# Transposes of values and of x1 moved inside the next projection, with a bank of their own for keys and values

## The chip, the core and the metric

The kernel runs on one core of one Trainium2 chip. The metric is the device time of one execution in microseconds. The kernel before took 1794.83 us (median of three runs, 1790.31 to 1797.67). Of the core's engines, TensorE (PE) multiplies and transposes and writes its results to PSUM, eight banks of 512 fp32 columns. VectorE (DVE) and ScalarE (ACT) read and write PSUM and SBUF, GpSimd (POOL) works in SBUF, and SyncE (SP) issues most DMAs. The engines run their own instruction streams and wait for each other by semaphores.

## The reference

Two layers, each added to its input. With x of shape (8, 512, 512), 16 heads of 64 columns, and one shared head of keys and values:

```python
# layer 0: attention with one head of keys and values
xn = layernorm(x, g_in)
q = (xn @ Wq).reshape(b, n, H, DH).transpose(0, 2, 1, 3) * scale     # Wq: 512 x 1024
k, v = split(xn @ Wkv)                                               # Wkv: 512 x 128
sim = mask(einsum('bhid,bjd->bhij', q, k) + bias)                    # null key and value in front
out = einsum('bhij,bjd->bhid', softmax(sim), v) -> (8, 512, 1024)
x1 = x + layernorm(out @ Wo, g_out)                                  # Wo: 1024 x 512
# layer 1: experts
logits = (x1 @ wt.T + cond @ wg.T) / 2                               # 8 experts, top 2
y = sum of the two chosen experts' outputs, weighted, + shared expert's output
result = x1 + y
```

## The kernel before

The program has stages, one behind the other, with a barrier between: project (to 267 us), attend (to 829 us), output (to 1103 us), then routing, experts and the shared expert. The change touches two of them. Products are made with fp32 operands split into a rounded high part and a rest, so each product is three matmuls (high x high, low x high, high x low).

**Project** (`stage_project`) goes over eight batches b. In SBUF, x of a batch is normalised by VectorE, with GpSimd for the reciprocal deviation. TensorE transposes it (`transpose_x`, L492) into two banks, chunks 0 and 1 first, and 2 and 3 once the banks are free again. ScalarE makes the high part of each chunk (L430), VectorE the rest (L341). Then TensorE makes nine output chunks n of 128 rows, twelve matmuls of 512 columns each (L531 to L533): n = 0 to 7 are queries, n = 8 is keys and values. They go round four banks (`proj_bank[n % 4]`), so keys and values share bank 0 with queries 0 and 4. ScalarE copies a query chunk (`q_hi`, L455), VectorE makes the rest (`q_lo`, L349), and SP stores both; there are two buffers for queries, so the copy of chunk n waits until the stores of chunk n - 2 have landed. ScalarE copies keys and values whole (`kv_out`, L461) and the keys' high part (`k_hi`, L464); VectorE makes `k_lo`. The values are needed transposed: `transpose_v` (L500) does it for batch b - 1 ahead of chunk 0 of batch b, right behind the first half of x's transposes for batch b + 1, and waits for both copies (`kv_copied`). VectorE's `copy_v` puts the result into `values`. The second half of x's transposes stands ahead of chunk 1 (`EARLY`). The masks' and biases' loads are issued by ScalarE between query copies.

**Output** (`stage_output`) goes over 32 tiles t of 128 rows. SP loads a tile of the attention's result (`o_in`), ScalarE and VectorE split it (`oT_hi` L1155, `oT_lo` L1106), and TensorE makes 24 matmuls of 512 columns into one of two banks (`project`, L1189 to L1191). VectorE takes the statistics (L1114, L1117), GpSimd the reciprocal deviation (L1088, L1091), VectorE normalises into `x1` (L1124), GpSimd multiplies by the gain and adds x (L1094, L1097), SP stores. For the logits x1 is transposed (`transpose_x1`, L1207), copied by ScalarE (`copy_x1T`, L1160, one buffer) and multiplied by the router's weights (`route`, L1213, 128 x 8 results). Ahead of the first tiles and of tile 30, ScalarE and VectorE also split the shared expert's weights (L1170, L1129).

All orders here are written by hand: what stands in a row in an engine's code is what it does in a row. TensorE's order of a step in the output stage is

```python
route(t - 2)                 # logits of x1 of tile t - 2
project(t, k)                # 24 matmuls
transpose_x1(t - 1, 1 - k)   # then ScalarE copies, and the next step begins with its route
```

Of the kernel before, what the change touches and what calls it, by code (L numbers as in the profile page):

```python
# [31 lines left out]
H, DH = 16, 64  # L32
# [120 lines left out]
def bank(psum, i):  # L153
    return psum[:, i * BANK:(i + 1) * BANK]
# [19 lines left out]
def stage_project(nc, x, fside, cond, mask, g_in, null_bias, Wq, Wkv, dram, psum, resident, wo_x1, ident, pow_half,  # L174
                  eps, spare, values, null_value):

    with ExitStack() as ctx:
# [42 lines left out]
        NP = IC + 1  # L220
        x_bank = [bank(psum, 0), bank(psum, 1)]
        proj_bank = [bank(psum, 2 + k) for k in range(4)]
        v_bank = bank(psum, 6)
        SMALL = 16 * 4


        EARLY, LATE = 1, 4
        AT_FIRST = (3, 5)

        block = ctx.enter_context(nc.Block())  # L230

# [84 lines left out]
        def _(dve):  # L316
# [46 lines left out]
                                  in1=null_value[:].unsqueeze(1).to_broadcast([P, TB, DH]), op=ALU.subtract  # L363
                                  ).then_inc(v_copied, 1)

            def step(b, k, before=True, split=True, norm=True):
                if split:
                    split_low(b + 1, 1 - k, range(0, 2))
                if before:
                    copy_v(b - 1)  # L370
                lower_q(b, range(0, EARLY))
                if split:
                    split_low(b + 1, 1 - k, range(2, DC))
                lower_q(b, range(EARLY, LATE))
                if norm:
                    measure(b + 2)
                lower_q(b, range(LATE, LATE + 1))
                if norm:
                    shift_and_scale(b + 2)
                lower_q(b, range(LATE + 1, IC))  # L380
                lower_k(b)
# [41 lines left out]
        def _(act):  # L423
# [16 lines left out]
            def copy_q(b, k, biases=None):  # L440
                first = isinstance(b, int) and b == 0
                for n in range(IC):
                    if first and n == 3:

                        act.wait_ge(x_loaded, 32)
                        for i in range(TB):
                            load_biases(i, 0)
                    if biases is not None and n % 4 == 3:
                        load_biases(2 * (1 - k) + n // 4, biases)
                    if n in (AT_FIRST if first else (0, EARLY)) and not (isinstance(b, int) and b + 1 >= B):  # L450
                        split_high(b + 1, 1 - k, range(0, 2) if n == (AT_FIRST[0] if first else 0) else range(2, DC))
                    act.wait_ge(proj_full, NP * b + n + 1)

                    act.wait_ge(q_stored[n % 2], 32 * (IC // 2 * b + n // 2))
                    act.activation(q_hi[:, n % 2, :], proj_bank[n % 4], ACT.Copy, scale=-float(DH) ** -0.5  # L455
                                   ).then_inc(q_hi_ready, 1)
                act.wait_ge(proj_full, NP * b + NP)

                act.wait_ge(vT_full, b)
                act.wait_ge(k_lo_ready, b)  # L460
                act.activation(kv_out[:], proj_bank[IC % 4], ACT.Copy).then_inc(kv_copied, 1)  # L461

                act.wait_ge(k_stored, 32 * b)
                act.activation(k_hi[:], proj_bank[IC % 4][0:DH, :], ACT.Copy).then_inc(kv_copied, 1)  # L464

            for j in range(2):
                act.wait_ge(wq_loaded[j], 16)
# [16 lines left out]
        def _(pe):  # L484
# [9 lines left out]

            def transpose_v(b):

                pe.wait_ge(kv_copied, 2 * b + 2)
                pe.wait_ge(v_copied, b)
                for t in range(TB):
                    last = pe.transpose(v_bank[:, t * P:(t + 1) * P], kv_out[:, t * P:(t + 1) * P], ident[:])  # L500
                last.then_inc(vT_full, 1)

            def project(b, k):
                first, has_next = isinstance(b, int) and b == 0, not (isinstance(b, int) and b + 1 >= B)
                if has_next and not first:
                    transpose_x(b + 1, range(0, 2))
                if not (isinstance(b, int) and b == 0):
                    transpose_v(b - 1)
                pe.wait_ge(xT_lo_ready, DC * b + DC)
                for n in range(NP):  # L510
                    if first and n in (0, IC // 2, IC):

                        pe.wait_ge(weights_lo, (0, IC // 2, IC).index(n) + 1)
                    if first and n == AT_FIRST[0]:
                        transpose_x(b + 1, range(0, 2))
                    if n == (AT_FIRST[1] if first else EARLY) and has_next:
                        transpose_x(b + 1, range(2, DC))

                    if n == 0:
                        pe.wait_ge(kv_copied, 2 * b)  # L520
                    elif n < 4:
                        pe.wait_ge(q_lo_ready, IC * b)
                    else:
                        pe.wait_ge(q_lo_ready, IC * b + n - 3)
                    if n < IC:
                        hi, lo = wq_hi[:, :, n * P:(n + 1) * P], wq_lo[:, :, n * P:(n + 1) * P]
                    else:
                        hi, lo = wkv_hi[:], wkv_lo[:]
                    out = proj_bank[n % 4]
                    for c in range(DC):  # L530
                        pe.matmul(out, hi[:, c, :], xT_hi[k][:, c, :], start=(c == 0), stop=False)  # L531
                        pe.matmul(out, hi[:, c, :], xT_lo[k][:, c, :], start=False, stop=False)
                        last = pe.matmul(out, lo[:, c, :], xT_hi[k][:, c, :], start=False, stop=(c == DC - 1))  # L533
                    last.then_inc(proj_full, 1)
# [423 lines left out]
def stage_output(nc, x, cond, wo_stage, wo_loaded, g_out, wt, wg, sw_gate, sw_up, sw_down, shared, dram, psum, ident,  # L958
                 pow_half, eps, spare, logits, x1_in, x1_loaded):

    with ExitStack() as ctx:
# [37 lines left out]
        WO_PARTS = [(0, 4), (4, IC)]  # L999

        WO_STARTS = [lo for lo, hi in WO_PARTS]

        SPLIT_AT = {0: 0, 1: 1, T - 2: 2}

# [144 lines left out]
        def _(act):  # L1149
# [12 lines left out]
            def step(t, k, m):  # L1162
                if not (known(t) and t + 1 >= T):
                    split_high(t + 1, 1 - k, m + k)
                if not (known(t) and t == 0):
                    copy_x1T(t - 1)
                if known(t) and t in SPLIT_AT:
                    n = SPLIT_AT[t]
                    act.wait_ge(shared_loaded[n], 16)
# [4 lines left out]
                act.activation(wo_hi[:, lo:hi, :], wo_part(j), ACT.Copy).then_inc(wo_hi_ready, 1)  # L1174
            split_high(0, 0, 0)
            steps(act, step)
            copy_x1T(T - 1)

        @block.tensor
        def _(pe):  # L1180
            def project(t, k):
                pe.wait_ge(oT_lo_ready, 2 * t + 2)
                if not (known(t) and t < 2):

                    pe.wait_ge(y_ready, t - 1)
                for c in range(IC):
                    if known(t) and t == 0 and c in WO_STARTS:
                        pe.wait_ge(wo_lo_ready, WO_STARTS.index(c) + 1)
                    pe.matmul(out_bank[k], oT_hi[k][:, c, :], wo_hi[:, c, :], start=(c == 0), stop=False)  # L1189
                    pe.matmul(out_bank[k], oT_hi[k][:, c, :], wo_lo[:, c, :], start=False, stop=False)  # L1190
                    last = pe.matmul(out_bank[k], oT_lo[k][:, c, :], wo_hi[:, c, :], start=False, stop=(c == IC - 1))  # L1191
                last.then_inc(out_full, 1)

            def group_logits():

# [19 lines left out]
                last.then_inc(logits_full, 1)  # L1215

            def step(t, k, m):
                if not (known(t) and t < 2):
                    route(t - 2)
                project(t, k)  # L1220
                if not (known(t) and t == 0):
                    transpose_x1(t - 1, 1 - k)
                if known(t) and t == 1:
                    group_logits()

            steps(pe, step)
            route(T - 2)
            transpose_x1(T - 1, 1)
            route(T - 1)
# [874 lines left out]
```

## Time and profile before

| | |
|---|---|
| runs | 1790.31, 1794.83, 1797.67 us |
| profiled execution, its own time | 1795.32 us |
| its span | 1793.6 us, mean clock of TensorE 0.967 |
| PE busy | 1631.7 us (91%), 10364 matmuls |
| DVE, ACT, POOL busy | 974.2, 714.9, 730.2 us |
| project stage, 53 to 267 us | PE busy 196.1 of 214 us |
| output stage, 866 to 1095 us | PE busy 206.06 of 229 us |

Matmuls are pipelined, so their durations overlap: the start of one to the start of the next is what it costs TensorE. The waits tell where it stands still and for whom. The granted clock is 1.00 at 2.4 GHz and 0.5 at 1.2 GHz; a stretch between has both.

### The profile page before, as it was taken

To read this page: it belongs to the slowest core of one execution; us is meant where nothing else is said; L and a number is where in the kernel's file an instruction comes from. 1 tells how busy PE (TensorE), PEld (TensorE's weight loads), DVE (VectorE), ACT (ScalarE), POOL (GpSimd) and SP (SyncE) were. 2 spreads that over 40 slices of the span, in tenths; PEclk is the share of its full clock that TensorE was granted. 3 is DMA by queue.
4 is the path that set the end of the run, shared out by engine and by line. 5 is a ranking of instruction groups with operands and counts; after the bars stand their busy time and mean duration, and the time that the engine had idled before them with its cause. 6 is when DMAs were issued, how large, how long until landed. Compare 5 with 4: busy or idle time off the path is not lost. (4 is left out here: it accounts for less than half of the span.)

```text
span 1793.6 us, 36160 instructions
## 1 busy us (share of the span) xinstructions
PE 1631.7 (91%) x10364; PEld 1362.8 (76%) x10365; DVE 974.2 (54%) x2442; ACT 714.9 (40%) x1823; POOL 730.2 (41%) x1177
## 2 busy tenths in 40 slices
PE   6899996999999999996988987989999999999998
PEld 4677775888888888885777776777777788778886
DVE  5444525776676676775554554653333333356555
ACT  3222324776676676774222121213333343321221
POOL 1000234675576676674554553142222222134222
PEclk9999998999999999998999998989999999989999
DMA  6566657776776766775444344015446633246333
GB/s 214 192 224 203 225 209 211 214 218 181 210 209 183 214 199 181 212 215 148 147 134 136 128 134 153 0 55 203 176 147 268 217 108 108 88 119 216 111 100 112
DMA packets 172361, 301.32 MB, mean 168 GB/s; under 512 B 16658, under 2 KB 64322, under 8 KB 170196
## 3 DMA queue, kind: packets, MB, share of 16 engines
q1 hardware_dynamic: 142324, 235.21, 41.1%
q0 software_dynamic: 11200, 35.73, 6.9%
q10 hardware_dynamic: 18720, 29.12, 4.7%
q8 instruction: 37, 0.61, 0.1%
q14 instruction: 80, 0.66, 0.1%
HBM read 186.99 MB, written 113.00 MB: 167 GB/s over the span
## 5 line engine op out<-in xcount | busy, mean ns | idle before, releaser
L754 POOL TENSOR_SCALAR probs<-probs,rsums 128x512 f32<-128x512 f32 (+3 forms) x512 | 264.0, 532 | 203.8 <-DVE rsums L790 203.4
L782 DVE CUSTOM_DVE_ANT_0 scores<-psum,resident 128x514 f32<-128x514 f32 (+3 forms) x512 | 243.2, 484 | 158.8 <-PE psum L897 136.9
L855 ACT ACTIVATE probs<-scores,lowest 128x514 f32<-128x514 f32 (+3 forms) x512 | 284.2, 557 | 34.1 <-DVE lowest L782 33.1
L909 PE MATMUL psum<-ident,probs 128*128 128x128 f32 x1280 | 235.1, 283 | 21.3 <-DVE probsT L797 14.0
L897 PE MATMUL psum<-keys,queries 128*128 (+4 forms) x640 | 222.6, 356 | 23.8 <-DMA queries_and_ones<-q_hi_d 17.8
L909 PEld LDWEIGHTS psum<-ident,probs 128*128 128x128 f32 x1280 | 152.3, 142 | 54.4 <-issue 39.5
L897 PE MATMUL psum<-keys_lo_and_mask,queries_and_ones 128*128 (+4 forms) x640 | 185.2, 298 | 0.0
L929 PE MATMUL psum<-probsT,v_now 128*64 128x128 f32 x2560 | 168.3, 278 | 0.9 <-DVE probsT L797 0.9
L897 PEld LDWEIGHTS psum<-keys,queries 128*128 128x128 f32 x640 | 127.7, 199 | 35.0 <-issue 21.0
L864 ACT ACTIVATE probsT<-psum 128x512 f32<-128x512 f32 (+2 forms) x192 | 93.6, 487 | 137.7 <-PE psum L909 120.2
L929 PEld LDWEIGHTS psum<-probsT,v_now 128*64 128x64 f32 x2560 | 137.4, 137 | 14.4 <-issue 1.6
L1806 PE MATMUL psum<-expert_weights,xT_hi 128*128 x284 | 122.4, 431 | 4.5 <-SPq L1694 4.0
L897 PEld LDWEIGHTS psum<-keys_lo_and_mask,queries_and_ones 128*128 128x128 f32 x640 | 125.8, 197 | 0.0
L797 DVE COPY probsT<-psum 128x512 f32<-128x512 f32 (+1 forms) x192 | 121.8, 635 | 3.8 <-PE psum L909 3.1
L1189 PE MATMUL psum<-wo_hi,oT_hi 128*128 128x512 f32 x256 | 105.2, 411 | 11.3 <-DVE oT_lo L1106 11.3
L1766 DVE TENSOR_TENSOR hT_lo<-psum,hT_hi 128x256 fp32r<-128x256 f32 x71 | 30.1, 424 | 157.0 <-ACT hT_hi L1723 157.0
L1808 PE MATMUL psum<-expert_weights,xT_lo 128*128 x284 | 112.8, 397 | 0.0
L1807 PE MATMUL psum<-expert_weights,xT_hi 128*128 x284 | 112.5, 396 | 0.0
L349 DVE SCALAR_TENSOR_TENSOR q_lo<-psum,q_hi 128x512 fp32r<-128x512 f32 x64 | 43.9, 687 | 125.2 <-ACT q_hi L455 125.2
L455 ACT ACTIVATE q_hi<-psum 128x512 fp32r<-128x512 f32 x64 | 38.3, 598 | 173.5 <-DMA q_lo_d<-q_lo 104.3
L531 PE MATMUL psum<-xT_hi,wq_hi 128*128 128x512 f32 x256 | 105.1, 411 | 1.6 <-DVE xT_lo L341 1.6
L138 POOL COPY slot_rows<-slot_tokens 128x1 int32 (+1 forms) x71 | 13.0, 183 | 224.0 <-PE psum L1801 221.6
(240 smaller groups left out, 3696.1 us busy)
## 6 DMA issues: line engine op xcount, KB each, us to landing
ys_d<-y_out ACTq DMA_DIRECT2D x71, 256.0 KB, 2.0
q_hi_d<-q_hi SPq DMA_DIRECT2D x64, 256.0 KB, 2.5
q_lo_d<-q_lo SPq DMA_DIRECT2D x64, 256.0 KB, 2.9
queries<-q_hi_d SPq DMA_DIRECT2D x64, 256.0 KB, 3.7
queries<-q_lo_d SPq DMA_DIRECT2D x64, 256.0 KB, 4.2
queries_and_ones<-q_hi_d SPq DMA_DIRECT2D x64, 256.0 KB, 4.5
oT_d<-o_out SPq DMA_DIRECT2D x64, 256.0 KB, 2.2
o_in<-oT_d SPq DMA_DIRECT2D x32, 512.0 KB, 3.9
```

What stands on the lines that cost most here:

```text
L531: pe.matmul(out, hi[:, c, :], xT_hi[k][:, c, :], start=(c == 0), stop=False)
L754: pool.tensor_scalar(out=row, in0=row, scalar1=rsums[:, n % RING:n % RING + 1], scalar2=1.0, op0=ALU.mult, op1=ALU.mult).then_inc(probs_sc ...
L782: dve.tensor_tensor_reduce(out=scores[n % 4][:, 0:CK[i]], in0=score_psum(n), in1=bias_of(resident, i, h), scale=1.0, scalar=3.0e38, op0=AL ...
L797: dve.tensor_copy(dst, src).then_inc(probsT_odd, 1)
L855: act.activation(probs[n % RING][:, 0:CK[i]], scores[n % 4][:, 0:CK[i]], ACT.Exp, bias=lowest[:, n % 4:n % 4 + 1], scale=-1.0, accum_out=s ...
L897: last = pe.matmul(whole[:, lo:hi], qs[hp % 2][:, n % 2, i * P:(i + 1) * P], ks[:, bass.ds((b % 2) * (AHEAD + S) + lo, hi - lo)], start=(p ...
L909: last = pe.transpose(probsT_bank[g % 2][:, at + j * P:at + (j + 1) * P], probs[n % RING][:, AHEAD + j * P:AHEAD + (j + 1) * P], ident[:])
L929: last = pe.matmul(o_bank[hp % 2][head * DH:(head + 1) * DH, cols], v_now[:, j * DH:(j + 1) * DH], probsT[half][:, at:at + P], start=(j == ...
L1189: pe.matmul(out_bank[k], oT_hi[k][:, c, :], wo_hi[:, c, :], start=(c == 0), stop=False)
L1806: pe.matmul(out, hi, experts[:, bass.ds(at, D)], start=start, stop=False)
L1807: pe.matmul(out, hi, experts[:, bass.ds(at + EW, D)], start=False, stop=False)
L1808: return pe.matmul(out, lo, experts[:, bass.ds(at, D)], start=False, stop=stop)
```

## The change

In the projection stage the transposes of batch b - 1's values go from the front of batch b to behind its second chunk (`VALUES_AT = 2`), and they wait for the first of the two key and value copies alone. Keys and values get bank 7. The waits for banks are written anew: a query chunk waits for the chunk that held its bank, across the batch's border too. VectorE's `copy_v` moves from the front of its step to behind the lowering of chunk 1.

In the output stage a tile's 24 matmuls are cut after 6 and after 15. In the first cut stand the transposes of x1 of tile t - 2 (before: of tile t - 1, behind the tile), in the second the logits of tile t - 2. ScalarE's copy follows. Behind the last tile come the transposes and logits of the last two.

```diff
-        v_bank = bank(psum, 6)
+        v_bank, kv_bank = bank(psum, 6), bank(psum, 7)
+        VALUES_AT = 2
 # VectorE, project stage
-                if before:
-                    copy_v(b - 1)
                 lower_q(b, range(0, EARLY))
                 if split:
                     split_low(b + 1, 1 - k, range(2, DC))
-                lower_q(b, range(EARLY, LATE))
+                lower_q(b, range(EARLY, VALUES_AT))
+                copy_v(b - 1)
+                lower_q(b, range(VALUES_AT, LATE))
 # ScalarE, project stage
-                act.activation(kv_out[:], proj_bank[IC % 4], ACT.Copy).then_inc(kv_copied, 1)
+                act.activation(kv_out[:], kv_bank, ACT.Copy).then_inc(kv_copied, 1)
-                act.activation(k_hi[:], proj_bank[IC % 4][0:DH, :], ACT.Copy).then_inc(kv_copied, 1)
+                act.activation(k_hi[:], kv_bank[0:DH, :], ACT.Copy).then_inc(kv_copied, 1)
 # TensorE, project stage
-                pe.wait_ge(kv_copied, 2 * b + 2)
+                pe.wait_ge(kv_copied, 2 * b + 1)
...
-                if not (isinstance(b, int) and b == 0):
-                    transpose_v(b - 1)
...
-
-                    if n == 0:
+                    if n == VALUES_AT and not (isinstance(b, int) and b == 0):
+                        transpose_v(b - 1)
+
+                    if n == IC:
                         pe.wait_ge(kv_copied, 2 * b)
-                    elif n < 4:
-                        pe.wait_ge(q_lo_ready, IC * b)
-                    else:
+                    elif not (isinstance(b, int) and b == 0 and n < 4):
                         pe.wait_ge(q_lo_ready, IC * b + n - 3)
...
-                    out = proj_bank[n % 4]
+                    out = proj_bank[n % 4] if n < IC else kv_bank
 # output stage
+        CUTS = [range(0, 2), range(2, 5), range(5, IC)]
 # ScalarE
-                if not (known(t) and t == 0):
-                    copy_x1T(t - 1)
+                if not (known(t) and t < 2):
+                    copy_x1T(t - 2)
...
             steps(act, step)
+            copy_x1T(T - 2)
             copy_x1T(T - 1)
 # TensorE; project() takes the chunks it makes, waits at the first and signals at the last
-            def project(t, k):
+            def project(t, k, chunks):
...
             def step(t, k, m):
+
+                project(t, k, CUTS[0])
+                if not (known(t) and t < 2):
+                    transpose_x1(t - 2, k)
+                project(t, k, CUTS[1])
                 if not (known(t) and t < 2):
                     route(t - 2)
-                project(t, k)
-                if not (known(t) and t == 0):
-                    transpose_x1(t - 1, 1 - k)
+                project(t, k, CUTS[2])
                 if known(t) and t == 1:
                     group_logits()
 
             steps(pe, step)
+            transpose_x1(T - 2, 0)
             route(T - 2)
             transpose_x1(T - 1, 1)
             route(T - 1)
```

TensorE at the border of two batches before, from the last matmul of keys and values on (line, operation, output and inputs, shape, and the semaphores it waits for; `kv_copied` is ScalarE's copies of keys and values, `xT_lo_ready` VectorE's rest of x):

```order
L533 MATMUL psum<-xT_hi,wkv_lo 128x512
L492 MATMUL psum<-ident,xin 128x128 [waits xT_lo_ready,xn_ready]
L492 MATMUL psum<-ident,xin 128x128 x3
L500 MATMUL psum<-ident,kv_out 128x128 [waits v_copied,kv_copied]
L500 MATMUL psum<-ident,kv_out 128x128 x3
L531 MATMUL psum<-xT_hi,wq_hi 128x512 [waits kv_copied,xT_lo_ready]
```

The same place in the changed kernel, and then the place ahead of its third chunk:

```order
L533 MATMUL psum<-xT_hi,wkv_lo 128x512
L494 MATMUL psum<-ident,xin 128x128 [waits xT_lo_ready,xn_ready]
L494 MATMUL psum<-ident,xin 128x128 x3
L531 MATMUL psum<-xT_hi,wq_hi 128x512 [waits q_lo_ready,xT_lo_ready]
...
L533 MATMUL psum<-xT_hi,wq_lo 128x512
L502 MATMUL psum<-ident,kv_out 128x128 [waits v_copied,kv_copied]
L502 MATMUL psum<-ident,kv_out 128x128 x3
L531 MATMUL psum<-xT_hi,wq_hi 128x512 [waits q_lo_ready]
```

The four transposes of `kv_out` went from ahead of the batch's first chunk to behind its second; the first chunk's wait is now for lowered queries.

TensorE in the loop of the output stage before, at the border of two tiles (`x` is x1, `x1T` its copied transpose, `oT` the attention's result):

```order
L1191 MATMUL psum<-wo_hi,oT_lo 128x512
L1207 MATMUL psum<-ident,x_1 128x128 [waits x1T_copied,x1_ready]
L1207 MATMUL psum<-ident,x_1 128x128 x3
L1213 MATMUL psum<-wt_T,x1T 128x8 [waits x1T_copied]
L1213 MATMUL psum<-wt_T,x1T 128x8 x3
L1189 MATMUL psum<-wo_hi,oT_hi 128x512 [waits y_ready,oT_lo_ready]
```

In the changed kernel, one tile from its first matmul on:

```order
L1192 MATMUL psum<-wo_hi,oT_hi 128x512 [waits y_ready,oT_lo_ready]
...
L1194 MATMUL psum<-wo_hi,oT_lo 128x512
L1211 MATMUL psum<-ident,x_0 128x128 [waits x1T_copied,x1_ready]
L1211 MATMUL psum<-ident,x_0 128x128 x3
L1192 MATMUL psum<-wo_hi,oT_hi 128x512
...
L1194 MATMUL psum<-wo_hi,oT_lo 128x512
L1217 MATMUL psum<-wt_T,x1T 128x8 [waits x1T_copied]
L1217 MATMUL psum<-wt_T,x1T 128x8 x3
L1192 MATMUL psum<-wo_hi,oT_hi 128x512
```

The transposes and the logits no longer stand next to each other: nine matmuls of the tile lie between them.

## Rows read from the trace of the kernel before

**Rows 1.** Who waited for whom, 0 to 300 us: us in total, times, longest.
```profile
PE psum L500 <- ACT k_hi L464: 14.7, 7, 4.0
ACT q_hi L455 <- DMA q_lo_d<-q_lo: 104.3, 34, 7.1
```
**Rows 2.** The same view, 866 to 1095 us.
```profile
PE psum L1213 <- ACT x1T L1160: 23.4, 30, 0.8
```
**Rows 3.** Busy time by stretch; PE, PEld, DVE, ACT, POOL, then clock, DMA share.
```profile
117.00:127.00 10.00, 6.11 (x26) 5.07 (x27) 3.38 (x6) 3.68 (x7) 0.00 (x0) 0.83 0.51 179
149.00:159.00 10.00, 7.41 (x37) 6.18 (x36) 3.77 (x7) 4.08 (x8) 0.00 (x0) 0.83 0.47 164
...
866.00:1095.00 229.00, 206.06 (x1046) 169.07 (x1046) 116.91 (x174) 48.32 (x87) 117.31 (x118) 1.00 0.41 134
```
**Rows 4.** PE in order of time at a border: start, duration, operation, idle before.
```profile
89.29 0.66 PE L500 MATMUL psum<-ident,kv_out 128*128 128x128 f32 x4 [2.55 <-ACT k_hi L464]
89.70 0.48 PE L531 MATMUL psum<-xT_hi,wq_hi 128*128 128x512 f32 x1
...
93.38 0.47 PE L531 MATMUL psum<-xT_hi,wq_hi 128*128 128x512 f32 x1
```
**Rows 5.** ScalarE in order of time at the same border.
```profile
87.68 0.60 ACT L455 ACTIVATE q_hi<-psum 128x512 fp32r<-128x512 f32 x1 [5.88 <-DMA q_lo_d<-q_lo]
...
89.13 1.25 ACT L430 ACTIVATE xT_hi<-psum,g_col 128x512 fp32r<-128x512 f32 x2
```
**Rows 6.** PE in order of time at the next border.
```profile
120.89 0.65 PE L500 MATMUL psum<-ident,kv_out 128*128 128x128 f32 x4 [4.00 <-ACT k_hi L464]
...
122.07 0.63 PE L533 MATMUL psum<-xT_hi,wq_lo 128*128 128x512 f32 x1
...
126.52 0.48 PE L531 MATMUL psum<-xT_hi,wq_hi 128*128 128x512 f32 x1
```
**Rows 7.** ScalarE at that border.
```profile
120.72 1.25 ACT L430 ACTIVATE xT_hi<-psum,g_col 128x512 fp32r<-128x512 f32 x2
```
**Rows 8.** VectorE at that border.
```profile
121.47 1.40 DVE L341 SCALAR_TENSOR_TENSOR xT_lo<-psum,g_col,xT_hi 128x512 fp32r<-128x512 f32 x2
```
**Rows 9.** PE in order of time over one tile of the output stage.
```profile
951.73 0.60 PE L1207 MATMUL psum<-ident,x 128*128 128x128 f32 x4
953.12 1.05 PE L1213 MATMUL psum<-wt_T,x1T 128*128 128x8 f32 x8 [0.80 <-ACT x1T L1160]
954.03 0.48 PE L1189 MATMUL psum<-wo_hi,oT_hi 128*128 128x512 f32 x1
...
959.39 0.39 PE L1191 MATMUL psum<-wo_hi,oT_lo 128*128 128x512 f32 x1
959.62 0.60 PE L1207 MATMUL psum<-ident,x 128*128 128x128 f32 x4
```
**Rows 10.** PE at the last border.
```profile
240.33 0.66 PE L500 MATMUL psum<-ident,kv_out 128*128 128x128 f32 x4 [1.16 <-ACT k_hi L464]
```
**Rows 11.** VectorE and GpSimd over the same tile as rows 9.
```profile
954.55 2.39 DVE L1106 TENSOR_TENSOR oT_lo<-o_in,oT_hi 128x512 fp32r<-128x512 f32 x2
956.48 1.63 POOL L1097 TENSOR_TENSOR x<-x,x_in 128x512 f32<-128x512 f32 x1
```
**Rows 12.** VectorE and PE, first tiles of the output stage and the last.
```profile
849.84 3.43 DVE L1106 TENSOR_TENSOR oT_lo<-o_in,oT_hi 128x512 fp32r<-128x512 f32 x2
...
858.11 3.45 DVE L1106 TENSOR_TENSOR oT_lo<-o_in,oT_hi 128x512 fp32r<-128x512 f32 x2
...
852.78 0.66 PE L1207 MATMUL psum<-ident,x 128*128 128x128 f32 x4 [2.43 <-POOL x L1097]
...
856.83 0.77 PE L1189 MATMUL psum<-wo_hi,oT_hi 128*128 128x512 f32 x1
...
867.25 0.47 PE L1189 MATMUL psum<-wo_hi,oT_hi 128*128 128x512 f32 x1
...
1093.53 0.60 PE L1207 MATMUL psum<-ident,x 128*128 128x128 f32 x4
```

More of the change, by code:

```diff
@@ L364, in copy_v, with step @@
                                   ).then_inc(v_copied, 1)
-            def step(b, k, before=True, split=True, norm=True):
+            def step(b, k, split=True, norm=True):
                 if split:
                     split_low(b + 1, 1 - k, range(0, 2))
-                if before:
-                    copy_v(b - 1)
                 lower_q(b, range(0, EARLY))
@@ L1180, in _ @@
         def _(pe):
-            def project(t, k):
[L1182 to L1186, printed above, removed]
+            def project(t, k, chunks):
+                if chunks[0] == 0:
+                    pe.wait_ge(oT_lo_ready, 2 * t + 2)
+                    if not (known(t) and t < 2):
+                        pe.wait_ge(y_ready, t - 1)
+                for c in chunks:
                     if known(t) and t == 0 and c in WO_STARTS:
@@ L1191, in project @@
                     last = pe.matmul(out_bank[k], oT_lo[k][:, c, :], wo_hi[:, c, :], start=False, stop=(c == IC - 1))
-                last.then_inc(out_full, 1)
+                if chunks[-1] == IC - 1:
+                    last.then_inc(out_full, 1)
             def group_logits():
@@ L1217, in step @@
             def step(t, k, m):
+                project(t, k, CUTS[0])
+                if not (known(t) and t < 2):
+                    transpose_x1(t - 2, k)
+                project(t, k, CUTS[1])
                 if not (known(t) and t < 2):
                     route(t - 2)
-                project(t, k)
-                if not (known(t) and t == 0):
-                    transpose_x1(t - 1, 1 - k)
+                project(t, k, CUTS[2])
                 if known(t) and t == 1:
```

## The prediction

> **What bounds the kernel now.** I read the shares per engine first, then who waited for whom, then the instructions in order of time around each wait. TensorE works 91% of the span, so what matters is where it does not. Two waits of it lie in the code that changes. In the projection stage it waits seven times, 14.7 us in all, for ScalarE's copy of the keys [rows 1]. In the output stage it waits for ScalarE's copy of the transposed x1, 23.4 us over thirty tiles, at most 0.8 us each [rows 2].
>
> Around a batch's end in the projection stage: TensorE has finished the keys and values, does eight transposes of x, and stands still (2.55 us at 89.29, 4.00 us at 120.89) [rows 4, 6]. It waits for the copy of the keys. On ScalarE that copy stands behind the last chunk of queries, which itself waited 5.88 us for a store to land [rows 5], because the two query buffers are emptied by stores (104.3 us of such waits) [rows 1]. So the lateness is made by the stores; TensorE only pays because the transposes of the values stand at the very front of the next batch. At two of the boundaries the granted clock averages 0.83 over the stretch, so part of it is at 1.2 GHz [rows 3]. A 512-column matmul behind such a stall lasts 0.63 us, at full clock 0.39 us, of which 0.233 us stand between one start and the next (twenty-four of them between 954.03 and 959.62) [rows 6, 9].
>
> In the output stage a tile takes 7.89 us (951.73 to 959.62): 5.59 us of matmuls, 1.39 us from the first transpose to the first logit matmul, 0.91 us of logit matmuls [rows 9]. Of the 1.39 us, the transposes need 0.41 us (the same four transposes of the values, 89.29 to 89.70) [rows 4]; the rest, 0.98 us, is the round trip over ScalarE's copy, during which TensorE has nothing else to do. The clock stays at 1.00 from 866 to 1095 [rows 3].
>
> **Projection stage.** Nothing is added to any engine; four transposes and one VectorE copy per batch move behind two chunks of queries, and the keys' copy has a bank of its own, so chunk 0 of the next batch waits for queries lowered long before, not for the keys. Now the first stall goes. What is late next? Chunk 1 still stands behind the second half of x's transposes. Those reuse the two x banks, so they wait until ScalarE and VectorE have split the first half, and ScalarE does that right behind the keys. So the loop that was (keys copied, values transposed, chunk 0, x transposes, chunk 1) becomes (keys copied, x split, x transposes, chunk 1), with chunk 0 beside it.
>
> Its length: ScalarE begins to split x at 120.72 [rows 7]; VectorE's first subtraction starts 0.75 us later and both take 1.40 us [rows 8]; then four transposes, 0.41 us. Chunk 1 starts 2.6 us after ScalarE begins the split. Before, it started 93.38 - 89.13 = 4.25 us after it [rows 4, 5] and at a boundary with half clock 126.52 - 120.72 = 5.8 us [rows 6, 7]. The gain is 1.65 us at each of three boundaries and 3.2 us at each of two: 11.3 us. TensorE still idles between chunk 0 and those transposes (at 120.89's boundary some 2.5 us, up to the end of the first subtraction at 122.2), so the clock may fall there still; I leave that in the range.
>
> Of the remaining two boundaries, the last has no x to transpose and saves its 1.16 us of idle [rows 10]. The first waits for x's own load, and I count it at nothing. The values' transposes are still done, and where TensorE sets the pace (the last two batches) they cost 0.41 us plus a restart: the first matmul behind other work lasts 0.48 us, one inside a run 0.39 us [rows 9]. That takes 0.5 us off twice, and adds 0.41 us back once at the last boundary. Sum for the stage: 11.3 + 1.16 + 0.4 - 1.0 = 11.9, say **12 us**. Elsewhere the transposes lie in TensorE's lead of up to three banks over the queries.
>
> This holds if the store-paced part of a batch (chunk 1 to chunk 7) keeps its length and only starts earlier. The x load is issued behind x's transposes, and the first query store behind it, so both move with the loop. If it doesn't hold, those boundaries give nothing (rival one). Ends for this stage: 2 us to 15 us. I take the value near the top since each term is read from rows and the DMA moves with its cause.
>
> The own bank adds no wait: it replaces bank 0 as the target of the keys and values, whose reader is the same copy. VectorE's copy of the values now stands behind the second chunk's lowering; by then the transposes are done, and VectorE has waits to spend it in.
>
> **Output stage.** x1 is transposed two tiles late inside the projection, six matmuls in, and the logits come nine matmuls later (2.1 us), while the round trip took 0.98 us. It is hidden. A tile then is 5.60 + 0.41 + 0.91 and one restart more, 0.1: **7.02 us**. The unknown is the price of a break in a run of matmuls with its own waits: from below 0 (weights of the logits could be loaded under the matmuls before, which they can't today), from above the 0.4 us that a whole set of transposes takes; near the restart row I take 0.1.
>
> Does another engine become the bound at 7.02? Counted from a tile's last matmul (about 951.9): VectorE has normalised it and split the tile after next by 954.55 + 2.39 = 956.94, 5.0 us later; GpSimd has x1 ready at 956.48 + 1.63 = 958.1, 6.2 us later, and its next tile's work starts about 1 us into the next period [rows 11]. Spare: 2.0 and 1.8 us. x1 is needed a whole tile later than before, so GpSimd's lateness no longer matters. ScalarE's order is a split, then the copy; its wait for x1's transposes ends 2 us into the tile and holds back only the next split, which waits for that tile's last matmul anyway. SP's loads follow the same VectorE and GpSimd events as before.
>
> The sum: from tile 3's first matmul (867.25) to tile 31's last (1093.5) before, 226.3 us [rows 9, 12]. After, 29 x 7.02 = 203.6: 22.7 us less. The start: tile 2 stood behind the transposes of x1 of tile 0, which waited 2.43 us for GpSimd (852.78), and began at 856.83, its first matmul lasting 0.77 us (half clock). It now goes straight on once its operands are split (853.3, the end of VectorE's split that started at 849.84). Then tile 3 is late next: VectorE finishes its split at 858.11 + 3.45 = 861.56, since the shared weights' split stands ahead of it [rows 12]. Tile 3 starts at 861.6 instead of 867.25: 5.6 us; a half-clock stretch in tile 2 would mostly hide in the 1.3 us that it otherwise waits. The tail behind tile 31 is the same (tile 31's x1 comes from GpSimd in either kernel). Stage: **28.3 us**, ends 16 (a tile at 7.44) and 33 (6.87).
>
> **Total.** 12 + 28.3 = 40.3 us. The profiled execution took 1795.3 us (span 1793.6 and 1.7 around it), 0.5 us over the median shown: 1795.3 - 40.3 = **1755 us**.
>
> **Rivals.** *One: the stores pace the projection.* For it: 104.3 us of waits for landings [rows 1]. Against: the DMA engines are busy about half of the time there (0.51 and 0.47) [rows 3]. Then only the last two boundaries pay, about 2 us: 1795.3 - 30.3 = 1765. The Trainium skill (Trainium Kernel Development and Optimization, Key Constraints) says that DMAs of all queues run on the same 16 engines and interleave. By that rule the bias loads on ScalarE's queue slow the query stores wherever both fall together, and an earlier TensorE helps less. The waits for landings agree with it, but the rule doesn't say that the stretch grows.
>
> *Two: the breaks cost more.* Each tile now has two breaks inside its projection, each with semaphore waits. At 0.4 us more per tile the output stage keeps 29 x 0.4 = 11.6 us: 1767. Against: the logits stand right before matmuls already, and cost those the 0.09 us above.
>
> *Three, slower: the clock.* If the chopped run of matmuls keeps the clock at 1.2 GHz, a tile's 5.59 us of matmuls [rows 9] come to twice that: 162 us over 29 tiles, 1917. It decides once a quarter of the matmuls (40.3/162) run so. Against: 1.00 over 229 us with an idle gap, transposes and 8-column matmuls together in every tile [rows 2, 3, 9]. The Trainium skill (TensorE: Matmul & The Clock Gate, Part 4: PE-mode transpose) says that transposes don't count as busy for the clock. By that rule the transposes placed inside the projection would speak for this rival. The trace doesn't bear it out: they stood beside the logits already and the clock held.
>
> *Four: the stalls only change place* (chunk 1's transposes wait as long as the keys did, and tiles wait for their split): about 1790.
>
> **Chances.** Forecast 0.71, rival one 0.13, two 0.10, three 0.03, four 0.03. The forecast's own range is 1746 to 1763. To hold 8 in 10 I reach to the first two rivals: 1745 to 1768. A change below 0.5% (9 us) can't be told from none. Faster by more: forecast, one and two, 0.94; same 0.03; slower 0.03.
>
> **What would show it.** No wait at the values' transposes; at x's second transposes in the batches 2 to 6 an idle of 0 to 3 us; the stage ends about 12 us sooner. A tile at 7.0 us, no wait at the logits; the clock at 1.00 from tile 3 on; tile 3 starting straight behind a VectorE split. Wrong if a tile takes over 7.3 us, if VectorE ends the waits in the steady tiles, or if the stretch from chunk 1 to chunk 7 grows by what the boundary lost.

## The result and the profile after

The changed kernel took 1752.21 us (median of four runs, 1749.6 to 1756.8), the kernel before in the same measurements 1796.25 us: a ratio of 0.9758, 95% interval 0.9719 to 0.9797. Forecast were 1755 us. The profiled execution's span is 1750.6 us, 43.0 us under the one before.

Where the 43.0 us lie can be read from four points that both traces have: the last copy of keys and values, the first matmul of the output stage, the last transposes of x1, and the end. Of the kernel before (ScalarE and PE in order of time):

```profile
266.24 0.60 ACT L461 ACTIVATE kv_out<-psum 128x512 f32<-128x512 f32 x1 [2.20 <-PE psum L533]
...
836.79 0.80 PE L1189 MATMUL psum<-wo_hi,oT_hi 128*128 128x512 f32 x1 [11.26 <-DVE oT_lo L1106]
...
1099.18 1.12 PE L1207 MATMUL psum<-ident,x 128*128 128x128 f32 x4 [3.31 <-POOL x L1097]
```

Of the changed kernel:

```profile
256.22 0.60 ACT L463 ACTIVATE kv_out<-psum 128x512 f32<-128x512 f32 x1 [2.21 <-PE psum L533]
...
824.25 0.79 PE L1192 MATMUL psum<-wo_hi,oT_hi 128*128 128x512 f32 x1 [11.26 <-DVE oT_lo L1107]
...
1052.98 1.11 PE L1211 MATMUL psum<-ident,x 128*128 128x128 f32 x4 [2.44 <-POOL x L1098]
```

| stretch | before | after | difference |
|---|---|---|---|
| start to the last copy of keys and values | 266.2 | 256.2 | -10.0 |
| to the first matmul of the output stage | 570.6 | 568.0 | -2.5 |
| to the last transposes of x1 | 262.4 | 228.7 | -33.7 |
| to the end | 694.4 | 697.6 | +3.2 |

The second and the fourth stretch run code that the change doesn't touch; over the traces of this study the second varies from 566 to 573 us and the fourth from 694 to 703 us. So the two stages that changed gave 43.7 us, and the other two stretches took 0.7 us of it back.

**Output stage.** Who waited for whom between 846 and 1045 us of the changed kernel has no row of TensorE left; its first rows are of the engines that wait for it, where [rows 2] had TensorE's 23.4 us:

```profile
ACT oT_hi L1156 <- PE psum L1194: 125.6, 28, 5.1
DVE stats L1115 <- PE psum L1194: 49.7, 29, 1.9
```

Busy time by stretch says the same: PE is busy all of the 199 us, at a granted clock of 1.00.

```profile
846.00:1045.00 199.00, 199.00 (x1047) 168.12 (x1047) 116.53 (x175) 51.43 (x86) 115.03 (x116) 1.00 0.46 151
```

A tile of the changed kernel, PE in order of time, against [rows 9]:

```profile
945.83 0.60 PE L1211 MATMUL psum<-ident,x 128*128 128x128 f32 x4
946.19 0.48 PE L1192 MATMUL psum<-wo_hi,oT_hi 128*128 128x512 f32 x1
...
948.35 0.95 PE L1217 MATMUL psum<-wt_T,x1T 128*128 128x8 f32 x8
949.15 0.48 PE L1192 MATMUL psum<-wo_hi,oT_hi 128*128 128x512 f32 x1
```

The next tile's transposes start at 952.69: 6.86 us a tile instead of 7.89. The logits take 0.80 us (948.35 to 949.15), not 0.91, and the transposes 0.36 us, not 0.41. The reason stands in the weight loads (PEld). Before, the first load of the logits' weights came with the copy, 0.01 us ahead of the matmul:

```profile
953.11 0.97 PEld L1213 LDWEIGHTS psum<-wt_T,x1T 128*128 128x128 f32 x8 [1.03 <-issue]
```

In the changed kernel it lies under the matmul before, 0.23 us ahead:

```profile
948.12 1.09 PEld L1217 LDWEIGHTS psum<-wt_T,x1T 128*128 128x128 f32 x8
```

**Projection stage.** TensorE no longer waits for the keys (one wait of 0.7 us for ScalarE's copy of keys and values is left). It waits at x's second transposes instead, 6.2 us in five waits (the view of who waited for whom, 0 to 300 us), where the kernel before had 1.0 us in one wait there and the 14.7 us of [rows 1]:

```profile
ACT q_hi L457 <- DMA q_lo_d<-q_lo: 100.5, 32, 7.0
PE psum L494 <- DVE xT_lo L343: 6.2, 5, 2.2
```

The border of [rows 4 and 5], ScalarE and PE of the changed kernel. Chunk 1 starts 2.61 us after ScalarE begins to split x (4.25 before; 2.6 forecast):

```profile
87.66 1.25 ACT L432 ACTIVATE xT_hi<-psum,g_col 128x512 fp32r<-128x512 f32 x2
...
89.29 1.22 PE L494 MATMUL psum<-ident,xin 128*128 128x128 f32 x8 [0.74 <-DVE xT_lo L343]
90.27 0.48 PE L531 MATMUL psum<-xT_hi,wq_hi 128*128 128x512 f32 x1
...
93.16 0.60 PE L502 MATMUL psum<-ident,kv_out 128*128 128x128 f32 x4
```

The next border, that of [rows 6 to 8], has a wait of 2.19 us there, and behind it matmuls of 0.63 us again: the clock fell.

```profile
119.22 1.31 PE L494 MATMUL psum<-ident,xin 128*128 128x128 f32 x8 [2.19 <-DVE xT_lo L343]
...
120.61 0.63 PE L532 MATMUL psum<-xT_lo,wq_hi 128*128 128x512 f32 x1
```

ScalarE's copies of queries give the stage batch by batch. From chunk 7's copy to the next batch's chunk 1's copy is the border; from there to chunk 7's copy is the store-paced stretch (us, from the starts of the copies):

| batch | border before | after | stretch before | after |
|---|---|---|---|---|
| 2 | 8.77 | 7.14 | 22.83 | 22.88 |
| 3 | 10.31 | 8.69 | 21.42 | 20.97 |
| 4 | 10.21 | 7.14 | 20.37 | 22.65 |
| 5 | 8.77 | 7.14 | 20.48 | 20.55 |
| 6 | 8.77 | 7.18 | (paced by TensorE) | |

Every border at full clock pays 1.6 us, as forecast, and batch 4's 3.1 us. Batch 3's pays 1.6 instead of 3.2 because the clock fell in both kernels. Batch 4's stretch grew by 2.3 us.

### The profile page after: what moved, and what is told of

The parts are those of the page before. It is cut to its first block and busy times, and to the rows that moved or that the text cites. A ratio compares the mean times of both kernels' runs of the same rounds, so it can differ in the third digit from the quotient of the medians.

```text
span 1750.6 us, 36162 instructions
## 1 busy us (share of the span) xinstructions
PE 1622.9 (93%) x10364; PEld 1357.3 (78%) x10365; DVE 972.0 (56%) x2442; ACT 719.0 (41%) x1823; POOL 730.9 (42%) x1177
## 5 line engine op out<-in xcount | busy, mean ns | idle before, releaser
L351 DVE SCALAR_TENSOR_TENSOR q_lo<-psum,q_hi 128x512 fp32r<-128x512 f32 x64 | 43.9, 687 | 113.4 <-ACT q_hi L457 113.4
```

## The experiments

Kernels of one chip share the runs of the kernel before; ratios are to those.

**One part alone.** The projection stage's code of one kernel and the rest of the other. The projection part alone:

```diff
 # stage_project as in the changed kernel; stage_output as in the kernel before
```

> Only the projection stage's part of the change (values later, own bank); the output stage is the one of before. Theory: 10 to 12 us less than before (changed kernel's trace: keys and values of the last batch copied at 256.2 us instead of 266.2), so about 1785, with the output stage's tile still at 7.88 us. Rival (the stores pace the stage): 2 to 5 us less. If the two parts touch one another (the clock, DMA phases), the two parts alone don't sum to the 43 us of both.

Measured: 1786.22 us, ratio 0.9946 (0.9926 to 0.9965). The output part alone:

```diff
 # stage_project as in the kernel before; stage_output as in the changed kernel
```

> Only the output stage's part (x1 transposed two tiles late inside the projection, logits nine matmuls behind). Theory: 33 us less than before, about 1762, a tile at 6.86 us as in the changed kernel, the projection stage unchanged. Rival (a part of the 33 us is the projection stage's doing, by another clock phase at the stage's start): under 30 us.

Measured: 1761.90 us, ratio 0.9816 (0.9793 to 0.9838), a tile at 6.87 us. The product of both ratios is 0.9763, both together gave 0.9758: within the intervals the parts add up, and no sign is left of one touching the other. The projection part's own profiled execution ended the stage at 260.43 us, only 5.8 us earlier. It was the slowest of this kernel's six. Two things differ from the trace above. Batch 5's stretch took 22.7 us, and at the border behind it TensorE waited 3.58 us at x's second transposes, with a mean clock of 0.83 over the ten microseconds around it:

```profile
209.04 1.31 PE L494 MATMUL psum<-ident,xin 128*128 128x128 f32 x8 [3.58 <-DVE xT_lo L343]
```

```profile
205.00:215.00 10.00, 6.41 (x27) 4.73 (x27) 6.30 (x7) 4.23 (x9) 2.63 (x4) 0.83 0.41 140
```

**Is it the bank or the place?** Keys and values back in the ring's first bank, the values' transposes still behind chunk 1:

```diff
-        v_bank, kv_bank = bank(psum, 6), bank(psum, 7)
+        v_bank, kv_bank = bank(psum, 6), proj_bank[IC % 4]
-                    if n == IC:
+                    if n == 0:
                         pe.wait_ge(kv_copied, 2 * b)
```

> The changed kernel with keys and values back in bank 0 of the four, so that chunk 0 of the next batch waits for the copies of keys and values again; the values' transposes stay behind chunk 1. Theory: chunk 0 then stands behind the copy as before, only the values' 0.4 us are out of the way, so the projection stage gives back 8 to 10 us of its 10 and the total is about 1761. Rival (moving the transposes is what pays, the bank nothing): 1752.

Measured: 1760.44 us, ratio 0.9814 (0.979 to 0.9838). TensorE waits for the keys again, now at chunk 0 (who waited for whom, 0 to 300 us):

```profile
PE psum L531 <- ACT k_hi L466: 11.0, 6, 3.0
```

All five borders (batches 2 to 6) lasted 8.4 us, against 8.8 before and 7.1 with the own bank, all at full clock: moving the transposes brings the 0.4 us that they last, the bank the other 1.2 us. The other order, the own bank with the transposes still in front, was not run. The total is the expected one, but its interval overlaps the changed kernel's, and the stage did not give back 8 to 10 us in the trace: it ended at 259.1 us, 2.9 us behind the changed kernel's. That execution was the fastest of the four (1757.05 us); batch 4's stretch took 20.2 us in it instead of 22.65, and the clock fell at none of its borders, although TensorE stood for 3.05 us at one (PE in order of time, and the stretch around it, clock 1.00):

```profile
117.91 0.50 PE L531 MATMUL psum<-xT_hi,wq_hi 128*128 128x512 f32 x1 [3.05 <-ACT k_hi L466]
```

```profile
112.00:122.00 10.00, 6.95 (x39) 5.68 (x38) 2.98 (x5) 3.60 (x7) 0.00 (x0) 1.00 0.74 262
```

**Distance or place?** The logits right behind the transposes, both inside the projection:

```diff
-        CUTS = [range(0, 2), range(2, 5), range(5, IC)]
+        CUTS = [range(0, 2), range(2, 2), range(2, IC)]
                     transpose_x1(t - 2, k)
-                project(t, k, CUTS[1])
                     route(t - 2)
```

> The changed kernel with the logits right behind the transposes of x1 (same two-tile lateness, same place inside the projection, no matmuls between). Theory: the round trip over ScalarE's copy stands open again, 0.95 to 1.05 us a tile, 7.85 us a tile and some 29 us more: about 1781. Rival (being two tiles late, or being inside the projection, is what pays): a tile stays at 6.9 to 7.1 us, under 1760.

Measured: 1781.61 us, ratio 0.9933 (0.9909 to 0.9958). The tile is back at 7.89 us (942.81 to 950.70), with the old wait:

```profile
942.81 0.60 PE L1211 MATMUL psum<-ident,x 128*128 128x128 f32 x4
944.19 1.05 PE L1217 MATMUL psum<-wt_T,x1T 128*128 128x8 f32 x8 [0.78 <-ACT x1T L1161]
950.70 0.60 PE L1211 MATMUL psum<-ident,x 128*128 128x128 f32 x4
```

And the other way round, transposes behind the tile as before (one tile late), only the logits inside the next projection:

```diff
                 project(t, k, CUTS[0])
-                    transpose_x1(t - 2, k)
                 project(t, k, CUTS[1])
                     route(t - 2)
                 project(t, k, CUTS[2])
+                    transpose_x1(t - 1, 1 - k)
 # ScalarE: copy_x1T(t - 1) in step t, as before
```

> The changed kernel with x1 transposed one tile late, behind the tile as in the kernel before, and only the logits inside the next projection. Theory: what pays is the distance between transposes and logits; x1 of a tile is ready 6.2 us behind the tile's last matmul and a tile takes 6.86 us, so there is 0.6 us to spare and the tile stays at 6.9 to 7.0 us, total 1752 to 1755. Rival (the two-tile lateness is needed, GpSimd's x1 would be waited for): 0.3 to 1 us more a tile, 1761 to 1780.

Measured: 1756.27 us, ratio 0.9771 (0.9745 to 0.9798), an interval that takes in the changed kernel's ratio; a tile at 6.85 us (943.79 to 950.64) and no wait of TensorE in the steady tiles:

```profile
943.79 0.60 PE L1210 MATMUL psum<-ident,x 128*128 128x128 f32 x4
947.67 0.95 PE L1216 MATMUL psum<-wt_T,x1T 128*128 128x8 f32 x8
950.64 0.60 PE L1210 MATMUL psum<-ident,x 128*128 128x128 f32 x4
```

So what a steady tile gains is the matmuls between transposes and logits, and nothing else of the edit: 27.4 of the stage's 33.7 us (from tile 3's first matmul on, 226.3 us before and 198.9 after). The two-tile lateness pays too, once, at the stage's start. Here, one tile late, the first transposes of x1 wait for GpSimd again as they did before [rows 12], tile 2 runs at half clock behind them, and tile 3's matmuls begin 30.4 us after the stage's first (at 824.52), where the kernel before had 30.5 us and the changed kernel has 24.2:

```profile
840.98 1.12 PE L1210 MATMUL psum<-ident,x 128*128 128x128 f32 x4 [2.43 <-POOL x L1098]
...
854.93 0.48 PE L1191 MATMUL psum<-wo_hi,oT_hi 128*128 128x512 f32 x1
```

From the first matmul to the last transposes this stage took 235.1 us, 6.4 us more than the changed kernel's 228.7. The totals are too close together to show it.

**What does a break cost?** Transposes and logits in two pairs each, a chunk apart:

```diff
-        CUTS = [range(0, 2), range(2, 5), range(5, IC)]
+        CUTS = [range(0, 2), range(2, 3), range(3, 5), range(5, 6), range(6, IC)]
 # between the cuts: transposes 0-1, transposes 2-3, logit products 0-1, logit products 2-3
```

> The changed kernel with the four transposes of x1 in two pairs, a chunk apart, and the four logit products in two pairs, a chunk apart: the same instructions, two more breaks in each tile's matmuls. Theory: a break costs about a restart, 0.08 to 0.1 us, since the weights behind it are loaded under the matmul before it; a tile takes 7.0 to 7.05 us instead of 6.86. Rival (a break with its wait costs 0.2 to 0.4 us): 7.3 to 7.7 us. Rival (the clock falls with a chopped run): granted clock under 1.00 in the output stage's steady tiles.

Measured in a single execution: 1751.4 us, a tile at 6.87 us (940.33 to 947.20), clock 1.00. Two more breaks cost 0.01 us together; the theory's 7.0 to 7.05 us was too high, and both rivals fall:

```profile
940.33 0.38 PE L1211 MATMUL psum<-ident,x 128*128 128x128 f32 x2
941.24 0.38 PE L1211 MATMUL psum<-ident,x 128*128 128x128 f32 x2
942.85 0.51 PE L1219 MATMUL psum<-wt_T,x1T 128*128 128x8 f32 x4
943.99 0.51 PE L1219 MATMUL psum<-wt_T,x1T 128*128 128x8 f32 x4
947.20 0.38 PE L1211 MATMUL psum<-ident,x 128*128 128x128 f32 x2
```

**Do the stores make the lateness?** The kernel before and the changed one with four query buffers:

```diff
-        q_hi, q_lo = sb("q_hi", [P, 2, S], F32R), sb("q_lo", [P, 2, S], F32R)
+        q_hi, q_lo = sb("q_hi", [P, 4, S], F32R), sb("q_lo", [P, 4, S], F32R)
 # n % 2 becomes n % 4 in copies, subtractions, stores and semaphores
-        wq_rest = sb("wq_rest", [P, DC, INNER // 2])
+        wq_rest = resident[:, rest:rest + at] ...      # a part that is loaded later
-        bias_loaded = [sem(f"bias_loaded{i}") for i in range(TB)]
+        bias_loaded = [sem(f"bias_loaded{i}") for i in range(TB // 2)]
```

> The kernel before with four instead of two buffers for the query halves (room made by staging the second half of Wq in a part of the bias array that is loaded later, and by two instead of four semaphores for the biases). Theory: the wait at the keys is late because the query copies wait for stores; with four buffers ScalarE follows TensorE, the wait at the values' transposes falls to about 1.2 us a batch, and the last keys and values are copied at about 255 us instead of 266: 1784. Rival (the DMA engines can't take the stores any faster): the waits for landings stay and the stage's end at 262 to 266.

> The changed kernel with the same four query buffers. Theory: TensorE alone sets the pace, 27.3 us a batch, no idle at x's second transposes; last keys and values at about 247 us instead of 256, total about 1743. Rival (DMA throughput): no faster than the changed kernel, 1750 to 1753.

Measured: the kernel before so changed 1776.68 us, ratio 0.9887 (0.9861 to 0.9912), the changed kernel 1741.85 us, ratio 0.9703 (0.968 to 0.9727). In the first, the waits for landings fall from 104.3 us [rows 1] to 3.1 us, and the wait for the keys from 14.7 to 3.8 us:

```profile
PE psum L501 <- ACT k_hi L465: 3.8, 7, 1.2
ACT q_hi L456 <- DMA q_lo_d<-q_lo: 3.1, 1, 3.1
```

The last copies of keys and values, first of the kernel before with four buffers, then of the changed one with four:

```profile
248.31 0.60 ACT L462 ACTIVATE kv_out<-psum 128x512 f32<-128x512 f32 x1 [2.21 <-PE psum L534]
```

```profile
243.09 0.60 ACT L464 ACTIVATE kv_out<-psum 128x512 f32<-128x512 f32 x1 [2.21 <-PE psum L534]
```

The stage of the kernel before ends 17.9 us sooner, 4 of them gained ahead of batch 1 already. The rival with the DMA engines' throughput falls: the same stores go out in less time, although a store's landing got no shorter (median 4.1 us for `q_lo` before and 4.6 us with four buffers, 3.9 and 3.7 us for `q_hi`, 85 to 205 us), and the engines' busy share rose from 0.65 to 0.71 (60 to 240 us). The edit also stages a part of Wq elsewhere and merges the biases' semaphores; that was not tested alone. With the lateness gone, the projection part of the change is worth 5.2 us (248.3 to 243.1) instead of 9 to 10. I had expected 255 us for the first: I took the 1.16 us of [rows 10] as what each border would keep, but x's transposes cover half of it at the other borders (3.8 us in seven). That explains some 4 of the 6.7 us; the rest I can't place. The changed kernel with four buffers takes 27.4 us a batch, as expected, its stage ends 4 us sooner than expected, and it is the fastest kernel of the study.

**Chunk 1 ahead of x's second transposes, too.**

```diff
-        EARLY, LATE = 1, 4
+        EARLY, LATE = 2, 4
```

> The changed kernel with x's second transposes ahead of chunk 2 instead of chunk 1. Theory: TensorE no longer idles between chunk 0 and those transposes, and the half-clock stretches there go, but the load of x and the first query store, which SP issues behind them, don't come sooner (at a late border the same, at an early one 1.6 us later), so the stage's end moves by -3 to +4 us: 1749 to 1756. Rival (TensorE's idle at the border is what the stage loses): 5 to 7 us less, 1746.

Measured: 1754.17 us, ratio 0.9756 (0.9729 to 0.9783), last keys and values at 251.9 us. No difference in the total; the stage's end is 4.3 us earlier than in the changed kernel's first trace, a little more than expected, but one of that code's six traces (see below) has it at 251.9 us too. The half-clock stretches are gone (1.00 at the borders of batches 2 to 6). Chunk 1 is copied 4.3 to 6.5 us behind chunk 7 (7.1 in the changed kernel at full clock), but the copy of chunk 2 then waits up to 8.49 us, for SP has the load of x and then the stores behind those transposes (ScalarE in order of time):

```profile
62.90 0.60 ACT L457 ACTIVATE q_hi<-psum 128x512 fp32r<-128x512 f32 x1 [2.11 <-PE psum L533]
...
73.15 0.60 ACT L457 ACTIVATE q_hi<-psum 128x512 fp32r<-128x512 f32 x1 [8.49 <-DMA q_lo_d<-q_lo]
```

**The first store ahead of the load of x.**

```diff
+                store_q(b, range(1))
                 sp.wait_ge(xT_full, DC * b + 2 * DC)
                 load_x(b + 2)
-                store_q(b, range(IC))
+                store_q(b, range(1, IC))
```

> The changed kernel with SP issuing the store of a batch's first queries ahead of the load of x instead of behind it. Theory: the first store lands sooner, so the copy of chunk 2 starts some 3.3 us behind that of chunk 1 instead of 4.8 us, but the load then falls on the next stores; what that leaves of the stage can't be told from the traces: the last keys and values copied between 250 and 260 us (four kernels with this projection code: 251.9 to 260.4). If the load of x were what makes the query copies wait, every batch gets about 1.5 us shorter and the end comes to 248 us or less.

> The changed kernel once more. Theory: boundaries as in its first trace (chunk 7's copy to the next chunk 1's copy 7.14 us at full clock), while one or two of the store-paced stretches of batches 4 and 5 last 2 us more or less than before and the clock falls at none to two borders; last keys and values between 251 and 261 us, total 1750 to 1755.

> The kernel with the first query store ahead of the load of x, timed beside the changed kernel on the same chip. Theory: 3 to 8 us less than the changed kernel (its first trace has the stage's end at 249.8 us), with the boundary's 7.1 us as they are. Rival (its first trace was a lucky one of the same spread): no difference, and the stage's end above 252.

Measured: 1747.24 us in a single execution; then beside the changed kernel 1750.17 us, ratio 0.9754 (0.9727 to 0.978), against 1754.76 us, ratio 0.9767 (0.9739 to 0.9796). The intervals overlap, so the totals don't tell. The traces tell more: the last keys and values were copied at 249.8 and 250.5 us, while six profiled executions with the changed projection code have 251.9, 256.2, 257.3, 257.5, 259.0 and 260.4, mean 257.0. The waits for landings are 78.7 us in the first of the two and 72.2 us in the second, in those six 98.2 to 113.4 us:

```profile
ACT q_hi L458 <- DMA q_lo_d<-q_lo: 78.7, 27, 5.9
```

By these two traces against six, the load of x ahead of the first store costs the stage some 7 us. It is not 1.5 us in every batch, though: the copy of chunk 2 starts 3.3 us behind that of chunk 1 in each, but batch 2's stretch is 4 us or more shorter (18.6 and 17.8 us instead of 22.3 to 22.9), and batch 3's is not. The repetition of the changed kernel behaved as expected in the stage (borders of batches 2, 4 and 5 at 7.1 us, batch 3's at 8.7 with the clock fallen, the stage's end at 257.5); its median of 1754.76 us is inside the expected range, single runs lay between 1747.8 and 1764.1.

## Why the prediction was right

The total was 1755 us, measured are 1752.2; by the profile it is 40.3 against 43.0 us. The mechanism held in both stages. That the total is this close is in part luck: the output stage gave 5.4 us more than forecast and the projection stage 2 us less, and the stretches that the change doesn't touch took back 0.7. By its steps:

- *The round trip over ScalarE is hidden, the distance does it.* Right for the steady tile; shown by the logits put close (7.89 us a tile) and by one tile's lateness being enough (6.85 us).
- *A tile takes 7.02 us.* The term that was mis-sized: 6.86 us, 0.16 x 29 = 4.6 us more gain. The added restart was right: the matmuls of a tile take 5.70 us, 0.1 more than before. Too long were the two other terms, 0.91 us for the logits (0.80) and 0.41 us for the transposes (0.36). Both came from rows behind a wait, where the weights are loaded with the first instruction; here they are loaded under the matmul before. Two more breaks cost 0.01 us.
- *Tile 3 starts at an unchanged VectorE split.* Tile 3's matmuls begin 24.2 us after the stage's first instead of 30.5: 6.3 us, forecast 5.6. The step is shown by the kernel that is one tile late, where this gain is gone (30.4 us). It was not the split that it waited for, which had ended at 848.0; tile 2 ran partly at half clock and ended just behind it, at 848.4. That the two hide one another was as forecast. How much is gained varies with the clock in tiles 1 and 2: in the other traces with the full change of the output stage tile 3 begins 24.4 to 27.0 us after the first.
- *The tail is the same.* Right: from tile 31's last matmul to the last transposes it is 5.88 us before and 5.89 after. In all 33.7 (6.3 + 27.4) against 28.3 us.
- *The border's loop.* Right to 0.05 us: 2.61 us from the split to chunk 1, 1.6 us less a border at full clock.
- *The stage gives 12 us.* It gave 10.0 here, 5.8 to 14.4 in six traces, 9.2 on average. Two terms were too high. I counted two borders as rid of their half clock, but the remaining wait at x's second transposes was followed by a fall of the clock at batch 3's in four of six traces (and at batch 6's in three, 3 us each); I had left that to the range. And batch 4's stretch grew by 2.3 us, which I had at nothing. In this trace 1.5 us gained ahead of batch 2, which I had at nothing too, made up for a part.
- *The store-paced stretch keeps its length* (rival one denies it). Mostly right: batch 2's and 3's kept theirs, while in five of six traces one of batches 4 and 5 is 0.8 to 2.3 us longer than before. Which collision of loads and stores does it was not isolated; it stays open.
- *Rivals.* One, as it was priced, fell with the changed kernel itself: the borders of batches 2 to 6 pay, and the stretches between them keep most of what they gain. What is true in it is that stores pace those stretches; the four buffers show that the time to land with only two buffers is the limit, not the engines' throughput. The share of about half that I set against it was read at two borders only; over the stage it is 0.65. Two and three (dear breaks, the clock) fell with the tile at 6.86 us and a clock of 1.00, and again with two added breaks. Four is true of 5.2 of the 14.7 us: the waiting at x's transposes went from 1.0 to 6.2 us.

## What to carry to other kernels

Where a transpose's result goes over another engine before the next matmul can use it, put enough independent matmuls between the two, even if a run has to be broken for it: breaks cost next to nothing here. Taking work a tile later still can pay where the first tiles wait for a slow producer. At a border, ask what the wait that you remove was late for: here it was stores into two buffers, and twice the buffers gave the kernel before 18 us in the stage, more than hiding the wait gave (with both, 1741.9 us). A load that is put ahead of a store in the same queue can be paid by whoever waits for that store: in batch 2 the copy of chunk 2 came 4.8 us behind that of chunk 1, and 3.3 us with the store first.

## What the runs showed of the hardware

A break in a run of 512-column matmuls cost next to nothing here: 6.87 us a tile with four breaks, 6.86 with two. The Trainium skill (TensorE: Matmul & The Clock Gate, Part 2: step 1, LDWEIGHTS) says that weight loads are pulled ahead of running matmuls; the trace agrees: the logits' first load starts 0.23 us ahead of their first matmul where it could start only with it before.

The clock's fall does not follow the idle's length alone. TensorE kept 2.4 GHz after standing 3.05 us and 2.41 us in the kernel with the shared bank, 2.55 us in the kernel before [rows 4] and 1.96 us in the changed one, and fell to 1.2 GHz after 1.91 us (projection part alone) and 2.19 us (changed kernel). What decides between them was not isolated.

Transposes inside the projection did not lower the clock: 1.00 over 199 us with every tile broken up. The Trainium skill (TensorE: Matmul & The Clock Gate, Part 4: PE-mode transpose) says that a transpose doesn't count as busy for the clock as a matmul does. No run here tests that by itself, since transposes take only 0.36 us of a tile's 6.86; but it was no reason here to keep them out of a run of matmuls, and rival three did not come.
